# A fused token mixer and feed-forward on one core: GpSimd's sums moved behind its low halves, the output sums moved to VectorE, the output chain one step sooner, the end cut in two halves of tokens, and the mixer's factors kept in PSUM

## The reference, cut to what matters

```
h = layernorm(x) * (1 + ca) + sa
x = x + ga * mixer(h)          # mixer: rms, qkv, rms of q and k, w = exp(k),
                               # cumsum(w*v) / cumsum(w) * sigmoid(q), gated unit, w_out, + h
h = layernorm(x) * (1 + cb) + sb
gate, up = h @ w_gu.T          # w_gu from 4-bit words, 2 x 1408 rows
y = (silu(gate) * up) @ w_down.T
x = x + gb * y / sqrt(mean(y * y) + 1e-6)
```

## Time and profile before

| what | value |
|---|---|
| median of 3 runs | 1942.83 us (1942.53 to 1943.8) |
| profiled execution, its own time | 1943.23 us |
| its span, first to last instruction | 1941.4 us |
| TensorE busy | 96% of the span |
| VectorE, ScalarE, GpSimd busy | 72%, 48%, 47% |
| mean granted TensorE clock | 0.992 |

### The profile page before, as it was taken

The page is one execution under the profiler, slowest core; times in us unless marked ns, Lnnn a source line. Parts: engine busy times, 40 slices in busy tenths (PEclk is TensorE's granted clock), DMA queues, the critical chain, the costliest instruction groups (busy, mean ns, idle before and its releaser), DMA issues. The chain is left out here.

```text
span 1941.4 us, 24528 instructions
## 1 busy us (share of the span) xinstructions
PE 1872.4 (96%) x8382; PEld 830.3 (43%) x8382; DVE 1399.3 (72%) x1787; ACT 924.8 (48%) x1414; POOL 909.7 (47%) x644
## 2 busy tenths in 40 slices
PE   6999999999999999999999999999999999999996
PEld 2443444444444444444444444444344444444442
DVE  6979768776867876877786686653677667767765
ACT  6753444235234434423533431221676766776673
POOL 2655435234314423422342331311768787777774
PEclk9999999999999999999999999999999999999998
DMA  8312220220202112021020121213210111011011
GB/s 309 130 55 65 76 70 24 75 66 18 81 20 70 51 40 69 11 87 60 24 74 17 48 66 33 88 39 113 118 44 22 44 66 59 8 66 66 1 44 65
DMA packets 70894, 120.44 MB, mean 62 GB/s; under 512 B 5024, under 2 KB 32672, under 8 KB 69152
## 3 DMA queue, kind: packets, MB, share of 16 engines
q1 hardware_dynamic: 70816, 119.45, 18.4%
HBM read 80.11 MB, written 39.32 MB: 62 GB/s over the span
## 5 line engine op out<-in xcount | busy, mean ns | idle before, releaser
L733 PE MATMUL bank<-Y,wsw 128*128 128x512 f16 x3072 | 689.9, 381 | 21.2 <-ACT late L939 14.4
L1140 POOL TENSOR_TENSOR late<-late 128x512 f16<-128x512 f32 x128 | 182.7, 1428 | 622.6 <-ACT late L947 621.9
L733 PEld LDWEIGHTS bank<-Y,wsw 128*128 128x128 f16 x3072 | 299.5, 98 | 394.6 <-ACT late L939 17.8
L2119 DVE SCALAR_TENSOR_TENSOR f_A<-bank,gu_s,f_A 128x512 f32<-128x512 f32 x352 | 259.9, 742 | 163.7 <-ACT f_A L1926 156.9
L708 PE MATMUL bank<-late,wout 128*128 128x512 f16 x1536 | 352.4, 379 | 0.4 <-POOL late L1140 0.4
L2008 POOL TENSOR_TENSOR f_A<-f_A 128x512 f32<-128x512 f32 x176 | 261.6, 1488 | 126.1 <-DVE f_A L2119 126.1
L1926 ACT ACTIVATE f_A<-bank,gu_s 128x512 f32<-128x512 f32 x336 | 229.1, 684 | 140.5 <-PE bank L1856 121.1
L1820 PE MATMUL bank<-f_HH,f_down_hi 128*128 128x512 f16 x704 | 266.8, 381 | 11.5 <-POOL f_HH L2025 11.2
L1206 DVE TENSOR_TENSOR late<-late,bank 128x512 f32<-128x512 f32 x128 | 87.3, 682 | 201.8 <-PE bank L733 192.7
L708 PEld LDWEIGHTS bank<-late,wout 128*128 128x128 f16 x1536 | 150.2, 98 | 188.8 <-issue 12.7
L939 ACT ACTIVATE late<-bank 128x512 f32<-128x512 f32 x128 | 76.4, 597 | 323.0 <-PE bank L733 279.4
(11 more groups left out here) (220 smaller groups left out, 2146.2 us busy)
## 6 DMA issues: line engine op xcount, KB each, us to landing
X<-xT SPq DMA_DIRECT2D x14, 1024.0 KB, 5.4
room<-packed SPq DMA_DIRECT2D x48, 176.0 KB, 2.4
h_scratch<-X SPq DMA_DIRECT2D x8, 1024.0 KB, 4.4
f_X<-x_scratch SPq DMA_DIRECT2D x8, 1024.0 KB, 5.5
x_scratch<-X SPq DMA_DIRECT2D x28, 256.0 KB, 2.2
h_scratch<-SQ SPq DMA_DIRECT2D x28, 256.0 KB, 2.2
outT<-f_X SPq DMA_DIRECT2D x7, 1024.0 KB, 4.3
room<-wswT SPq DMA_DIRECT2D x4, 1024.0 KB, 6.5
```

The costliest lines, as they stand in the source:

```text
L733: mm = nc.tensor.matmul(out[:], wsw[:, pw, k, col:col + P], Y[:, px, k, :], start=(k == 0 and pw == 0 and px == 0), stop=(k == DT - 1 and ...
L1140: nc.gpsimd.tensor_tensor(UG[:, j % 2, 1, :], G, UG[:, j % 2, 0, :], ALU.subtract).then_inc(UG_low, 1)
L2119: nc.vector.scalar_tensor_tensor(a, EV[ev_bank(j, m, steps)][:], gu_s[:, which * I_T + j, g:g + 1], a, ALU.mult, ALU.add).then_inc(by_dve, 1)
```

## The change

In the mixer `DEV`, the place of the factors, becomes PSUM for three of the four kinds (`RD` is left for k alone), and `n_sqrt` and `n_scale` work in `N_BANK` in place of `RS2`. The scans of every block read the ones from PSUM: from block 1 on a new ScalarE copy (`s2_ones`, one per block, at step 3) fills the bank of q's factor once that is used up. Waits of the matmuls that reuse those banks move accordingly.

In the feed-forward the tables change: in block 0 the sums of GpSimd go from places 8, 10, 12 and 22, 24, 26 to 8, 11, 12 and 23, 24, 27 (so behind `low` at the fourth place of a step); two of the four `scale_n` and two of the high halves go to later places; the low halves of that norm go into block 1. The output chain starts and ends a step sooner; `result` moves from GpSimd (places 31, 35, 39, 43) to VectorE (33, 36, 37, 40), and a copy waits for its own tile of `down` alone. In the last step VectorE adds the up halves and makes the low half instead of GpSimd; the squares start tile by tile, VectorE adds them in pairs so that two matmuls are left of four, the table of the square root is loaded ahead, and reciprocal, norm, result and store run over the first and then the second 256 tokens.

```diff
-        RD = sb("RD", [P, 2, T], F32)
+        RD = sb("RD", [P, T], F32)
-        DEV = {VAR: RD[:, 0, :], HSQ: RD[:, 0, :], KSQ: RD[:, 1, :], QSQ: HR[:]}
+        DEV = {VAR: R_BANK[VAR][:], HSQ: R_BANK[HSQ][:], KSQ: RD[:, :], QSQ: R_BANK[QSQ][:]}
...
-                nc.scalar.activation(RS2[:], N_BANK[:], ACT.Sqrt, bias=eps[:, 0:1]).then_inc(n_root, 1)
+                nc.scalar.activation(N_BANK[:], N_BANK[:], ACT.Sqrt, bias=eps[:, 0:1]).then_inc(n_root, 1)
...
+            def s2_ones(b):
+                if isinstance(b, int) and b == 1:
+                    act.wait_ge(root[1], 4)
+                else:
+                    act.wait_ge(q_norm, DT * (b + 1))
+                nc.scalar.activation(RUN_BANK[1][:], run[:], ACT.Copy).then_inc(run_ready, 1)
...
                     if s2 and j == 3:
+                        s2_ones(b + 1)
                         s2_exp_q(b + 1)
...
-                    if first:
-                        dve.wait_ge(run_ready, 1)
-                    nc.vector.tensor_tensor_scan(buf[:, c, :], RUN_BANK[:] if first else run[:], buf[:, c, :],
+                    dve.wait_ge(run_ready, b + 1)
+                    nc.vector.tensor_tensor_scan(buf[:, c, :], RUN_BANK[0 if first else 1][:], buf[:, c, :],
...
-            return range(4, 8) if first(b) else range(5, 6)
+            return range(4, 8) if first(b) else range(4, 5)
...
-        ADD_X, MEAN, CENTRE, SQUARE_N, ADD_N, VARIANCE = 8, 16, 17, 19, 22, 30
-        INVERT_N, SCALE_N, HIGH_N, LOW_N = 32, 36, 38, 40
+        ADD_X = {8: 0, 11: 1, 12: 2}
+        ADD_N = {23: 0, 24: 1, 27: 2}
+        SCALE_N = {36: 0, 37: 1, 40: 2, 41: 3}
+        HIGH_N = {38: 0, 39: 1, 42: 2, 43: 3}
+        LOW_N = {0: 0, 1: 1, 4: 2, 5: 3}
-        COPY_Y = {8: 0, 9: 1, 10: 2, 11: 3}
-        RESULT = {31: 0, 35: 1, 39: 2, 43: 3}
+        COPY_Y = {6: 0, 7: 1, 8: 2, 9: 3}
+        SQUARE_Y = {9: 0, 10: 1, 11: 2, 12: 3}
+        ADD_Y = {11: 0, 12: 1, 15: 2}
+        Y_MEAN, Y_ROOT = 18, 19
+        INVERT_Y = {20: 0, 22: 1, 23: 2, 24: 3}
+        NORM_Y = {25: 0, 28: 1, 29: 2, 32: 3}
+        RESULT = {33: 0, 36: 1, 37: 2, 40: 3}
...
-                act.wait_ge(down_used, I_T * (b + 1))
+                act.wait_ge(out_done, DT * b + c + 1)
...
-            act.wait_ge(down_used, I_T * NB)
+            nc.scalar.activation(table[:], eps[:, 2:3], ACT.Sqrt)
             act.wait_ge(y_sum, NSUM * (NB - 1))
             for c in range(DT):
+                act.wait_ge(out_done, DT * (NB - 1) + c + 1)
                 nc.scalar.activation(SQY[:, c, :], O[c][:], ACT.Square).then_inc(y_squared, 1)
...
+            last_up()
             hidden(NB - 1, I_T - 1)
-            for c in range(DT):
-                invert_y(NB - 1, c)
-            dve.wait_ge(out_ready, DT * (NB - 1))
-            norm_y(NB - 1, 0, O[0][:])
-            for c in range(1, DT):
-                norm_y(NB - 1, c, O[c][:])
-                result(NB - 1, c - 1)
-            result(NB - 1, DT - 1)
+            last_hidden_low()
+            for n in range(DT // 2):
+                add_squares(n)
+            for i in range(len(PARTS)):
+                invert_part(i)
+                for c in range(DT):
+                    norm_part(i, c)
+            for c in range(BY_POOL, DT):
+                result_part(1, c)
```

More of the change, by code:

```diff
@@ L270, in mixer @@
         low_bits = sem("low_bits")
-        decode = [sem(f"decode{i}") for i in range(6)]
+        decode = [sem(f"decode{i}") for i in range(5)]
         decoded = sem("decoded")
@@ L1042, in _ @@
             act.wait_ge(root[0], 3)
-            nc.scalar.activation(RUN_BANK[:], run[:], ACT.Copy).then_inc(run_ready, 1)
+            nc.scalar.activation(RUN_BANK[0][:], run[:], ACT.Copy).then_inc(run_ready, 1)
             split(PU[0])
@@ L1560, in _ @@
             inverse(VAR, 0)
-            dve.wait_ge(ca_ready, 1)
+            dve.wait_ge(c_silu, 3)
             early_scale(0)
@@ L1724, in opened @@
             return by_act, (DT * I_T - len(OPENS)) * b + DT * j + m // 2 + 1 - skipped
-        def now(place, start, step=1):
-            n = (place - start) // step
-            return (place - start) % step == 0 and 0 <= n < DT, n
         def slot_free(eng, done, b, j):
@@ L1808, in down @@
             def down(b, j, c):
+                last = isinstance(b, int) and (b, j) == (NB - 1, I_T - 1)
                 if c == 0:
@@ L1872, in _ @@
             pe.wait_ge(*opened(NB - 1, I_T - 1, GROUPS - 2))
-            for c in range(DT):
-                pe.wait_ge(y_squared, DT * (NB - 1) + c + 1)
-                mm = nc.tensor.matmul(R[:], ones[:], SQY[:, c, :], start=c == 0, stop=c == DT - 1)
+            for c in range(0, DT, 2):
+                pe.wait_ge(last_dve, ADDED + c // 2 + 1)
+                mm = nc.tensor.matmul(R[:], ones[:], SQY[:, c, :], start=c == 0, stop=c == DT - 2)
             mm.then_inc(y_red, 1)
@@ L1938, in beside_first @@
             def beside_first(place):
-                due, c = now(place, SQUARE_N)
-                if due:
-                    square_n(c)
-                due, c = now(place, HIGH_N)
-                if due:
-                    split(c)
+                if place in SQUARE_N:
+                    square_n(SQUARE_N[place])
+                if place in HIGH_N:
+                    split(HIGH_N[place])
                 if place == VARIANCE:
@@ L2028, in beside_first @@
             def beside_first(place):
-                due, n = now(place, ADD_X, 2)
-                if due and n < NSUM:
-                    add_x(n)
-                due, n = now(place, ADD_N, 2)
-                if due and n < NSUM:
-                    add_n(n)
+                if place in ADD_X:
+                    add_x(ADD_X[place])
+                if place in ADD_N:
+                    add_n(ADD_N[place])
             def beside(b, place):
@@ L2038, in beside @@
                     add_y(b - 1, ADD_Y[place])
-                if place in RESULT:
-                    result(b - 1, RESULT[place])
             for b in range(NB):
@@ L2055, in _, with result_part @@
                             beside(b, DT * j + i)
-                    half(b, j, 1)
-            low(NB - 1, I_T - 1)
+                    if not (isinstance(b, int) and (b, j) == (NB - 1, I_T - 1)):
+                        half(b, j, 1)
+            def result_part(i, c):
+                pool.wait_ge(res_loaded, 16 * NB)
+                pool.wait_ge(y_norm, DT * (NB - 1 + i) + c + 1)
+                nc.gpsimd.tensor_tensor(X[:, c, PARTS[i]], X[:, c, PARTS[i]], Y[:, c, PARTS[i]], ALU.add).then_inc(out_ready, 1)
+            for c in range(DT):
+                result_part(0, c)
+            for c in range(BY_POOL):
+                result_part(1, c)
         @block.vector
@@ L2128, in beside_first @@
             def beside_first(place):
-                for start, work in ((CENTRE, centre), (INVERT_N, invert_n), (SCALE_N, scale_n), (LOW_N, low_n)):
-                    due, c = now(place, start)
-                    if due:
-                        work(c)
+                for places, work in ((CENTRE, centre), (INVERT_N, invert_n), (SCALE_N, scale_n)):
+                    if place in places:
+                        work(places[place])
                 if place in MIXER_RESULT:
@@ L2136, in beside @@
             def beside(b, place):
-                for places, work in ((INVERT_Y, invert_y), (NORM_Y, norm_y)):
+                if b == 1 and place in LOW_N:
+                    low_n(LOW_N[place])
+                for places, work in ((INVERT_Y, invert_y), (NORM_Y, norm_y), (RESULT, result)):
                     if place in places:
```

141 lines of the change are left out of this document (95 added, 46 removed).

## The result

| | before | after |
|---|---|---|
| median of 4 runs | 1943.12 us (1942.53 to 1943.8) | 1924.66 us (1923.0 to 1925.18) |
| ratio, 95% interval | | 0.9903, 0.9888 to 0.9918 |
| profiled execution, its span | 1941.4 us | 1922.9 us |

A forecast was written before the change was run, and what follows sets the result against it. TensorE, busy 96% of the span, was taken as the bound, so only its waits, slow running and ends could give time: 3.5 + 4.5 + 5.5 + 6.6 = 20.1 us off 1943.2, so 1923.1, median 1922.7; range 1916 to 1930.

The forecast's parts named there:

- Part 1: Mixer: factors and ones in PSUM speed VectorE's scans, so the 4.0 us silu wait shrinks; 3.5 us, bounds 0 to 5.9.
- the prediction's own bound: Mixer: TensorE can keep no more than VectorE's chain gains, as VectorE's products hold it again some 20 us later; 3.5 us taken.
- rival E: Mixer and feed-forward blocks 1 to 7: slow matmuls go for good, no wait is left; 1918 us, chance 10%.
- rival B: Mixer gives nothing: the contended modulation still waits for the weight split; 3.5 us less gain, 1926.2 us, chance 24%.
- Part 2: Feed-forward block 0: sums behind low halves 2.6 us, scalings and low halves moved 1.9 us; 4.5 us, bounds 2 to 5.5.
- Part 3: Feed-forward blocks 1 to 7: results off GpSimd end a 0.72 us wait per block; 5.5 us, bounds 1.5 to 6.9.
- the prediction's own rule: TensorE's waits: each costs its idle time and 0.38 - 0.215 = 0.17 us more.
- Rival C: Feed-forward blocks 1 to 7: earlier, denser output chain costs 0.8 us a block, what results saved; 1930.6 us, chance 14%.
- Rival A: Feed-forward: the 28 results moved to VectorE collide with GpSimd halves, TensorE waits 0.7 us each; 1951 us, chance 4%.
- Part 4: The end: shorter chain after the last take, less TensorE idle time, clock stays 1.00, halves of tokens; 6.6 us.
- the signs that the prediction put down: Mixer: no wait near 171 us, scans at 1.19; feed-forward blocks 1 to 7: at most 0.2 to 0.3 near place 16.
- D: Whole kernel: hardly any change, waits turn up elsewhere and the clock still falls at the end; 1942 us, chance 4%.

The follow-up runs named there:

- e3: Changed kernel with the results of feed-forward blocks 1 to 7 back on GpSimd, output chain left early; 1931.1 us, ratio 0.9940.
- e4: Changed kernel with GpSimd's sums ahead of its low halves again in feed-forward block 0; 1925.36 us, ratio 0.9911.
- e7: Changed kernel with one GpSimd weight split in the mixer's iteration 0 moved from step 5 to step 4; 1919.88 us, ratio 0.9883.
- e13: Changed kernel with block 0's layer-norm scalings and low halves back at places 36 to 39 and 40 to 43; 1925.85 us, ratio 0.9910.
- e5: Changed kernel with the output chain of blocks 1 to 7 a step later, results still on VectorE; 1924.82 us, ratio 0.9908.
- e9: Changed kernel with GpSimd's three output-chain sums a step apart, each behind a low half, and what follows later; 1922.54 us, ratio 0.9893.
- e10: Changed kernel with the edits of e7 and e9 together, results at places 37, 38, 40 and 41; 1919.13 us, ratio 0.9875.
- e6: Changed kernel with the last step's up halves and low half given back to GpSimd; 1924.91 us, ratio 0.9907.
- e12: Changed kernel with the end's reciprocal, norms, results and stores over all 512 tokens at once, on VectorE; 1923.99 us, ratio 0.9900.

## Why the prediction was right, and where it was off

The sum was 20.1 us and the traces show 18.6. No part of the sum failed as a mechanism, but one term was mis-sized.

**Part 1, 3.5 us predicted, 2.0 measured: the mis-sized term.** Of its working, the scans held (4.80 us for four), and TensorE's later stop behind the products did hand part back. What did not was "It then reaches the modulation 3 us sooner, about as GpSimd's split also comes sooner". Counted from the first gated-unit matmul, the V scans end at 44.58 in place of 46.94, 2.4 sooner; then a product (`hidden`) waits 0.46 for TensorE, and the modulation that is held up starts at 50.72 in place of 52.51, 1.8 sooner. As it lasts as long as before, the first wait shrank by 1.8 and not by 4.0, and TensorE goes on behind the later products at 79.64 in place of 81.42, again 1.8 sooner. So the prediction's own bound held, that TensorE keeps no more than what VectorE's chain gains; that gain was half of what I took. The other 0.2 of the 2.0 comes later in the mixer and was not traced. The slow matmuls did not go either: 24 take 6.94 us behind a wait of 2.21 (7.75 before), against a pace of 5.34; but e3 and e4 show that they cost nothing here (last section), so rival E's gain from them was not there to be had. This is rival B's argument, that the contended instruction is not one whose operand is moved, at half its price; e7 shows that it was the right place to look, since freeing that instruction is worth 3.9 us more.

**Part 2, 4.5 predicted, 4.3 measured** (e4, e13). The 0.2 of a wait that I left twice behind the sums did not come; instead one of 0.26 stands behind the scalings. The DMA wait at the first `down`, 0.38 us longer than the wait that it replaces, was not foreseen.

**Part 3, 5.5 predicted, 6.2 measured:** blocks 2 to 6 fell from 69.31 to 68.43 on average, 0.88 a block in place of 0.78. e3 and e5 show the cause as given, the engine of the results. The wait at place 16 came where it was put, but for another reason: not ScalarE's density but a sum beside `hidden`, which e9 removes. The number is near in part by luck. By the prediction's own rule that wait of 0.26 costs 0.26 + 0.17 = 0.43 a block and not 0.2, so the gain must be 1.3 a block and not 0.98: e3 gives 1.03 of it to the results, and the rest are pauses too short for the list. Rival C, that the denser chain eats the gain, falls with e5. Rival A, collisions of the results, falls for two reasons: the longest result takes 1.11 us here, and where one takes 1.76 in every block (e10) TensorE has no wait of 0.7 for it.

**Part 4, 6.6 predicted, 6.2 measured.** VectorE's up and low halves give 1.1 (e6) and the two halves of tokens 0.5 (e12). Read from the traces, not tried: no result ahead of those halves 0.9 (2.02 of idle time less 1.1), and the clock 1.7 (12 matmuls in about 2.75 us instead of 4.4). The 2.0 left are the squares tile by tile, their pair sums and the square root's table, which were not tried apart. The square root starts 8.4 us after the last take's end, as worked out; the 0.4 that is missing lies behind it, where the last result ends after 16.9 us and not 16.5. GpSimd's half results took 0.72 each, near the lower bound of 0.63.

Of the signs that the prediction put down, two did not come: the wait near 171 us stayed, at 2.2, and the scans take 1.26 and not 1.19. Its working has a few slips that change nothing above. The modulation in the earlier trace rows does not end with GpSimd's split but 0.55 us behind it (168.54 against 167.99), which is about its own length without a neighbour, 0.68. The lower bound of part 3 is 7 x 0.18 = 1.3 and not 1.5. The chance of a clear gain, all but A and D, is 0.92 and not 0.93.

## What to carry to other kernels

Where VectorE and GpSimd stop each other, moving one operand to PSUM pays twice: for the instruction itself, and because other GpSimd work can now be put beside it; the second was the larger here (3.9 us against 2.0), and it took one number in a table. Count a freed wait only up to the next engine that its chain meets: here TensorE gained what VectorE's chain gained, whatever its own matmuls did in between. Look at every long pair in the stretch before crediting the gain to one of them. A median hides collisions; but a collision costs only where another engine waits for what it delays. Judge steps of a microsecond or two by the time of a block in the trace, and compare executions that started alike, since here the program's start alone moved profiled executions by more (the first gated-unit matmul stood between 109.6 and 112.4 us).
